# The product of the K-V sums and Wo in three f16 passes, in a one-core graph transformer layer

## What is computed

```python
xn = _layernorm(x)                                  # x: (1250, 1024)
q = relu(xn @ Wq + bq); k = relu(xn @ Wk + bk); v = xn @ Wv + bv      # 16 heads of 64
context = einsum('bhlk', q, k) / (l * 64)           # no softmax
attn = einsum('bhlk,bhkd->bhld', context, v)
mix = attn @ Wo + bo
x = x + gnn(xn) + mix                               # gnn: two graph layers over 20000 edges
x = x + ffn(_layernorm(x))                          # two quantized linear layers, gelu between
```

## Time and profile before

| | us |
|---|---|
| median of 3 runs | 1299.38 (1298.27 to 1300.58) |
| the profiled execution, whole | 1298.98 |
| its span from first to last instruction | 1297.2 |
| PE busy | 1289.7 (99%) |
| DVE busy | 848.6 (65%) |
| ACT busy | 652.1 (50%) |

### The profile page before, as it was taken

How to read it: one execution, slowest core, us unless ns; L and a number is a source line. 1 busy time by engine, 2 the same in 40 slices (tenths; PEclk the granted TensorE clock), 3 DMA queues, 4 the chain that set the end, 5 groups by cost and what they waited for, 6 DMA issues and landing times.

```text
span 1297.2 us, 18782 instructions
## 1 busy us (share of the span) xinstructions
PE 1289.7 (99%) x6370; PEld 615.0 (47%) x6370; DVE 848.6 (65%) x1472; ACT 652.1 (50%) x895; POOL 98.4 (8%) x91
## 2 busy tenths in 40 slices
PE   9999999999999999999999999999999999999999
PEld 5454445555545444444444444444444444444444
DVE  6854552362567778975992664246987978786774
ACT  7766565354312336632441763446863277465460
POOL 0000000000000001100000010133550100000000
PEclk9999999999999999999999999999999999999999
DMA  9487987864235366724877899999949829732523
GB/s 357 146 274 264 290 271 206 296 226 155 89 114 195 142 212 224 215 86 156 279 255 251 178 254 221 259 293 320 306 148 377 262 64 291 181 69 81 130 60 103
DMA packets 203094, 269.10 MB, mean 207 GB/s; under 512 B 110465, under 2 KB 144001, under 8 KB 199425
## 3 DMA queue, kind: packets, MB, share of 16 engines
q1 hardware_dynamic: 191008, 260.12, 63.5%
q0 software_dynamic: 1440, 5.24, 2.2%
q10 hardware_dynamic: 10560, 2.62, 1.3%
HBM read 184.33 MB, written 57.67 MB: 187 GB/s over the span
## 4 chain that ended last, share of the span: by engine, by line
PE 86%; DVE 6%; DMA 5%; ACT 2%; issue 1%; SPq 0%; DVEq 0%; ACTq 0%
PE ps L2366 32%; PE ps L2688 13%; PE ps L2647 12%; PE ps L2497 8%; PE ps L2768 7%; PE ps L2805 7%; PE ps L2566 3%; DMA SPLIT<-in_Wself 1%; DMA Zb<-blocks_scratch 1%; PE ps L2505 1%; PE ps L2418 1%; DVE AM L2179 1%; DMA S<-HL 1%; PE ps L2400 1%; DVE S L1859 1%
## 5 line engine op out<-in xcount | busy, mean ns | idle before, releaser
L2366 PE MATMUL ps<-S,XH 128*128 128x512 f16 x1440 | 316.7, 379 | 0.5 <-DVE Zb L1766 0.5
L2366 PEld LDWEIGHTS ps<-S,XH 128*128 128x128 f16 x1440 | 140.5, 98 | 164.4 <-DVE Zb L1766 0.6
L2366 PE MATMUL ps<-S,Zb 128*128 128x512 f16 x480 | 106.4, 379 | 0.0
L2497 PE MATMUL ps<-XH,S 128*128 128x512 f16 (+1 forms) x576 | 102.6, 339 | 0.0
L2366 PE MATMUL ps<-Zb,XH 128*128 128x512 f16 x432 | 94.8, 379 | 0.0
L1059 ACT ACTIVATE AT<-ps 128x320 f16<-128x320 f32 x40 | 17.4, 435 | 142.2 <-PE ps L2366 142.1
L1719 DVE TENSOR_SCALAR STREAM<-tables,keys 128x320 f16 x240 | 71.5, 298 | 23.5 <-PE ps L2566 13.3
L2647 PE MATMUL ps<-XH,AT 128*128 128x512 f16 x400 | 86.7, 379 | 0.0
L2647 PE MATMUL ps<-Zb,AT 128*128 128x512 f16 x400 | 86.5, 379 | 0.0
L2497 PEld LDWEIGHTS ps<-XH,S 128*128 128x128 f16 x576 | 56.1, 98 | 47.0 <-issue 2.3
L2366 PEld LDWEIGHTS ps<-S,Zb 128*128 128x128 f16 x480 | 46.9, 98 | 54.4 <-issue 0.6
(11 more groups left out here) (330 smaller groups left out, 1998.4 us busy)
## 6 DMA issues: line engine op xcount, KB each, us to landing
STREAM<-in_w_all SPq DMA_DIRECT2D x48, 512.0 KB, 5.5
STREAM<-in_w1t SPq DMA_DIRECT2D x42, 512.0 KB, 5.4
STREAM<-in_w2t SPq DMA_DIRECT2D x28, 512.0 KB, 5.1
XIN<-in_x SPq DMA_DIRECT2D x20, 512.0 KB, 5.1
Zb<-in_w1t SPq DMA_DIRECT2D x14, 512.0 KB, 7.3
blocks_scratch<-S SPq DMA_DIRECT2D x4, 1792.0 KB, 8.5
blocks_scratch<-STREAM SPq DMA_DIRECT2D x4, 1792.0 KB, 8.8
S<-blocks_scratch SPq DMA_DIRECT2D x7, 1024.0 KB, 11.4
```

The costliest lines, as they stand in the source:

```text
L2366: last = mm(acc[:, n * BANK:(n + 1) * BANK], left(l, kc), right(kc, r)[:, n * BANK:(n + 1) * BANK], start=(kc == 0 and i == 0), stop=(kc = ...
L2497: last = mm(ps[:, 3 * j * BANK + a:3 * j * BANK + b], Wq_s[:, kc, l, mc], XH[:, r, kc, a:b], start=(kc == 0 and l == 0 and r == 0), stop=( ...
```

## The change

- Wo is brought chunk by chunk through the two slots of `SPLIT` (`wo_loads`) in place of one 4 MB transfer, and split to f16 halves in `S1` by ACT (`wo_hi`) and DVE (`wo_lo`): chunks 0 and 1 ahead of Q chunk 0, 2 and 3 behind the copies to `kvT`, 4 and 5 behind Q chunk 1, 6 and 7 behind `w1_sum` on DVE and behind the means of Q chunk 1 on ACT.
- `kvT` is split too, in one piece, into `kv_parts` in `HL`, by a scale `kv_s` from its norm. ACT does its half behind the four means of Q chunk 2, DVE its half ahead of Q chunk 3.
- `m_pe` runs three f16 passes, six matmuls in place of two f32 ones. It waits for all of Wo's halves (`split_lo` 32) and both halves of `kvT` (`kvT` 17). M's own split uses the constant 2^-15.
- M(5), M(6) and M(7) move into the first U tile, ahead of its chunks 1, 2 and 4; banks and waits follow. The counts of `split_lo` that later loads wait for rise by eight.

The core of the diff:

```diff
-            sp.wait_ge(S("v_ps"), NT)
-            sp.dma_start(Wo_raw, Wo.rearrange("(k p) n -> p k n", p=P)).then_inc(S("wo_in"), 16)
+            def wo_loads(first):
+                for kc in range(first, first + 2):
+                    load_split(Wo, kc, kc % 2, 24 + kc)
+            wo_loads(0)
+            wo_loads(2)
...
-            mean_loads(0, Q_FIRST, HC)
+            for n in range(2):
+                for j in range(4):
+                    mean_load(0, Q_FIRST + 4 * n + j, j)
+                wo_loads(4 + 2 * n)
...
+            act.wait_ge(S("scales"), 4)
+            act.wait_ge(S("v_ps"), NT)
+            wo_hi(0)
             for m in range(3):
                 q_hi(m, m % 2)
...
-                if m == 2:
+                if m < 2:
+                    wo_hi(2 + 2 * m)
+                else:
                     norm("norm_m", 1, 5)
                 q_means(m)
-            act.wait_ge(S("a_m"), 1)
+                if m == 1:
+                    wo_hi(6)
+            act.wait_ge(S("kv_s"), 1)
+            A(kv_parts[:, 0, :], kvT, ACT.Copy, scale=col("kv_s")).then_inc(S("kv_hi"), 1)
...
+            wo_lo(2)
             q_dve(1, 1)
+            wo_lo(4)
...
             V.tensor_reduce(col("w1_sum"), MW[:, 0, :], AXX, ALU.add).then_inc(S("w_sum"), 1)
+            wo_lo(6)
...
+            dve.wait_ge(S("kv_hi"), 1)
+            V.scalar_tensor_tensor(kv_parts[:, 1, :], kvT, col("kv_s"), kv_parts[:, 0, :],
+                                   ALU.mult, ALU.subtract).then_inc(S("kvT"), 1)
             q_dve(3, 1)
...
-                for n in range(2):
-                    last = mm(ps[:, (bank + n) * BANK:(bank + n + 1) * BANK], kvT[:, p * P:(p + 1) * P],
-                              Wo_raw[:, p, n * BANK:(n + 1) * BANK], start=True, stop=True)
+                for i, (l, r) in enumerate(((0, 0), (0, 1), (1, 0))):
+                    for n in range(2):
+                        last = mm(ps[:, (bank + n) * BANK:(bank + n + 1) * BANK], kv_parts[:, l, p * P:(p + 1) * P],
+                                  Wo_s[:, p, r, n * BANK:(n + 1) * BANK], start=(i == 0), stop=(i == 2))
...
-            pe.wait_ge(S("wo_in"), 16)
+            pe.wait_ge(S("split_lo"), 32)
+            pe.wait_ge(S("kvT"), 17)
...
+            u_first = {1: lambda: m_late(5), 2: lambda: m_late(6), 4: lambda: m_late(7), 7: q_and_m_done}
```

More of the change, by code:

```diff
@@ L42 @@
 W_SCALE = 2.0 ** 14
+M_DOWN = 2.0 ** -15
 XW = X_SCALE * W_SCALE
@@ L117, in gps_kernel @@
             ln_std=1, ln_rstd=1, p=8, s=8, sq0=1, sq1=1, norm_kv0=1, norm_kv1=1, a_kv0=1, a_kv1=1, c_kv0=1, c_kv1=1,
-            sq_q=2, norm_q=2, sq5=5, norm5=5, bq=KC, bq2=KC, bqs=KC, a_q=1, c_q=1, kv_sq=1, w1_sum=1, norm_m=1, a_m=1,
+            sq_q=2, norm_q=2, sq5=5, norm5=5, bq=KC, bq2=KC, bqs=KC, a_q=1, c_q=1, kv_sq=1, w1_sum=1, norm_m=1, kv_s=1, a_m=1,
             c_u=1, inv=1, tmp=1, to_pos=1,
@@ L151, in gps_kernel @@
         Wv_tail = Zb[:, 2 * KC * D:2 * KC * D + 4 * D].bitcast(F32).rearrange("p (k n) -> p k n", k=2)
-        Wo_raw = S1[:, :].bitcast(F32).rearrange("p (k n) -> p k n", k=KC)
+        Wo_s = weight(S1)
+        kv_parts = HL[:, 0, :, :]
         qT = Zb[:, :].rearrange("p (h k n) -> p h k n", h=2, k=KC)
@@ L505, in u_moves @@
                 if split:
-                    load_split(Wself0, t, j, 24 + t)
+                    load_split(Wself0, t, j, 32 + t)
                 sp.wait_ge(S("u"), t + 1)
@@ L562, in _ @@
                 if t + 2 < KC:
-                    load_split(Wneigh0, t + 2, t % 2, 34 + t)
+                    load_split(Wneigh0, t + 2, t % 2, 42 + t)
                 sp.wait_ge(S("s0"), t + 1)
@@ L577, in prep_load @@
                 if n == 0:
-                    sp.wait_ge(S("split_lo"), 40)
+                    sp.wait_ge(S("split_lo"), 48)
                 elif n == 1:
@@ L1021, in m_hi @@
                 alone(act)
-                A(M_s[:, p, 0, :], banks(bank), ACT.Copy, scale=col("a_m")).then_inc(S("m_hi"), 1)
+                A(M_s[:, p, 0, :], banks(bank), ACT.Copy, scale=M_DOWN).then_inc(S("m_hi"), 1)
             def q_act(m, j):
@@ L1027, in q_act, with wo_hi @@
                 q_means(m)
+            def wo_hi(first):
+                for kc in range(first, first + 2):
+                    split_chunk(Wo_s, kc, kc % 2, 24 + kc, at("s", WO))
+            act.wait_ge(S("scales"), 4)
+            act.wait_ge(S("v_ps"), NT)
+            wo_hi(0)
             for m in range(3):
@@ L1602, in q_dve, with wo_lo @@
                                        ALU.max, ALU.subtract).then_inc(S("q_lo"), 1)
+            def wo_lo(first):
+                for kc in range(first, first + 2):
+                    split_chunk(Wo_s, kc, kc % 2, 24 + kc, at("s", WO))
+            wo_lo(0)
             q_dve(0, 0)
@@ L1674, in _ @@
             w_mean(0, ps[:, MEAN_AT + 1:MEAN_AT + 2])
[L1675 to L1679, removed]
+            pow2(col("kv_s"), col("norm_m"))
+            link(V.reciprocal(col("kv_s"), col("kv_s")))
+            V.tensor_scalar(col("kv_s"), col("kv_s"), W_SCALE, None, ALU.mult).then_inc(S("kv_s"), 1)
+            dve.wait_ge(S("kv_s"), 1)
+            times(col("a_m"), col("kv_s"), at("s", WO), M_DOWN)
             c = col("c_u")
@@ L1696, in qm_dve @@
                 q_dve(m, j)
-                m_dve(m - 3, 0 if isinstance(m, int) and m == 7 else 6)
+                m_dve(m - 3, 6)
             made = dve.alloc_register("made")
@@ L2533, in _ @@
                 qm_pe(m, m % 2)
[L2534 to L2540, removed]
+            pe.wait_ge(S("q_t"), 7)
+            pe.wait_ge(S("q_lo"), 7)
             pe.wait_ge(S("pad0"), 1)
@@ L2586, in counts_between, with m_late, q_and_m_done @@
                 return {kc: at_place(kc) for kc in {*places, *more}}
+            def m_late(p):
+                if p == 5:
+                    pe.wait_ge(S("q_t"), 8)
+                elif p == 7:
+                    pe.wait_ge(S("m_lo"), 5)
+                m_pe(p, M_BANK[p])
+            def q_and_m_done():
+                pe.wait_ge(S("q_lo"), 8)
+                pe.wait_ge(S("m_lo"), 8)
+            u_first = {1: lambda: m_late(5), 2: lambda: m_late(6), 4: lambda: m_late(7), 7: q_and_m_done}
             def u_pe(t):
                 wait(pe, "u", t - 1)
-                if t == 0:
-                    pe.wait_ge(S("m_lo"), 5)
                 product(banks(4 * (t % 2)), lambda l, p: qT[:, l, p, tile_of(t)], of(M_s), 0 if t == 0 else None, "m",
-                        counts_between(t, {7: lambda: pe.wait_ge(S("m_lo"), 8)} if t == 0 else {}))\
+                        counts_between(t, u_first if t == 0 else {}))\
                     .then_inc(S("u_ps"), 1)
@@ L2605, in s0_pe @@
                         between=counts_between(NT + t)).then_inc(S("s0_ps"), 1)
[L2607 removed]
+            pe.wait_ge(S("split_lo"), 40)
             pe.wait_ge(S("u"), 9)
@@ L2628, in deg_pe @@
                 last.then_inc(S("deg_ps"), 1)
-            pe.wait_ge(S("split_lo"), 40)
+            pe.wait_ge(S("split_lo"), 48)
             for t in range(8):
```

19 lines of the change are left out of this document (8 added, 11 removed).

## The result

The changed kernel took 1301.38 us (median of 12 runs, 1300.90 to 1304.60), the kernel before in the same sessions 1299.07 (12 runs, 1297.29 to 1300.58). The ratio is 1.0020 with a 95% interval of 1.0012 to 1.0027: **slower by 2.3 us**, 1.6 to 3.5, inside the forecast range of 1298.2 to 1303.6 and 0.4 over the forecast time. The profiled execution took 1302.64, 1.3 over the median, with a span of 1300.5, 3.3 over that of the kernel before.

What follows compares the result with a forecast made beforehand. PE, busy 99% of the span, was taken as the bound. M's gain of 3.5 us, stalls of 5.0 and a late landing of 0.1 summed to +1.6: 1301.0 us against the median, range 1298.2 to 1303.6.

Steps and rivals of the forecast that it cites:

- M's cost: M blocks on PE: 1.29 us each in place of 1.73, a gain of 3.5 us over all eight.
- The first stall: PE at total(5) in Q: waits 2.5 us for w1_sum, behind two low halves of Wo on DVE.
- The second stall: PE ahead of M(0): waits 2.5 us for kvT's halves; M(0) starts at 291.2, 5.0 later with both stalls.
- Landing of Wo chunks 6 and 7: Wo loads in Q: they land about when DVE wants their high halves; 0.1 us taken as cost.
- The rival of a late landing, (c): Wo chunk 7 in Q lands late, up to 3.8 us, giving 1304.7; chance 15%.
- The clock: PE's granted clock behind the stalls: no fall, cost taken as 0 between 0 and 14 us; a fall had 6%.
- The start of U: U's first tile: M(7) done at T (Q chunk 7's end) + 13.0, asked at T + 14.2; cost 0.
- The sum: Whole kernel: -3.5 + 5.0 + 0.1 = +1.6 us, 1301.0 against the median.
- behind U everything hangs on PE, so the shift stays as it is: Kernel behind U: PE's delay of +1.6 us is carried unchanged to the end.
- same: Whole kernel: measured within 2.6 us of no change, 1296.8 to 1302.0; chance 71%.
- (d): PE's clock falls behind one or both stalls in Q: 1.3 to 14 us more, most likely 2 to 4; chance 6%.

Runs made afterwards that it cites:

- the last pair: p_before_total against a repeat of p_after with total(5) and M(0) moved later and the count waiting for M's sixth low half: 1296.76 and 1293.32 us.
- p_total_late: p_after with total(5) and its wait for w1_sum moved 3.2 us later, into Q chunk 3: 1302.85 us.
- p_u_undone: p_after with M(5) to M(7) ahead of U again, in the banks of the kernel before: 1301.33 us.
- p_after: The changed kernel with its 74 transposing transfers replaced by plain ones of the same rows: 1301.08 us.
- p_count_6: p_after with the wait ahead of U's first count for M's sixth low half in place of its eighth: 1299.52 us.
- p_before: The kernel before the change with its 74 transposing transfers replaced by plain ones of the same rows: 1297.57 us.
- p_before_total: p_before with total(5) and its wait moved 3.2 us later, into Q chunk 3: 1296.76 us.
- the third change: On p_after with total(5) and M(0) moved later, the wait ahead of U's count is for M's sixth low half: 1293.50 us with all three.
- p_m0_late: p_after with M(0) and its waits moved 6.3 us later, into Q chunk 4: 1299.82 us.

## Why the prediction held, and where it didn't

**M's cost** was right: 1.29 per block in the profile, 3.44 in all by the last pair.

**The first stall** was right in place, releaser and size: 2.5 expected, 2.58 measured, total(5) at 275.8 expected and 275.82 measured. The step that found it was the comparison of two rows of different engines, 273.13 and 273.28, where neither showed a wait. The agreement to 0.02 us is partly luck: the chain begins one step ahead of where the prediction took it up, at ACT's first mean, which started at 259.83 here and at 259.86 in the kernel before, but up to 1.6 later in other profiles.

**The second stall** was right in what counts, 291.2 expected for M(0) and 291.26 measured, and p_total_late shows that the chain is the one that was added up. Its own size was wrong, 0.79 and not 2.5, because of the clock: 1.4 of the difference is Q chunk 3, 0.2 total(5) itself.

**Landing of Wo chunks 6 and 7** was right: ACT had made the last high half by 276.33, half a us before DVE came to it. The two low halves took 2.73 in place of 2.48, but no wait is in it: one of the two operations itself lasted 1.54 us, the other 1.27, and why stays open. The rival of a late landing didn't come about for these two; but the w1 means of p_u_undone show that a late transfer at the head of the chain delays PE directly.

**The clock** was wrong. It was a rival at 6%, with "I take 0, since the only row with idle PE time shows none". All six profiles with a stall of over 2 us in Q show the low level behind it, those without one don't. The row with 1.13 us of idle time in the earlier trace rows was too far from 2.5 to say anything. The Trainium skill, "TensorE: Matmul & The Clock Gate", section "HAM oscillation — how this bites in real kernels", warns of gaps in the matmul stream behind which the clock is granted at half. The traces agree that it happens (0.50 behind each of the six stalls), but four of these stalls, 2.25 to 2.74 us, are shorter than the gaps that its rule names; here the measurement decides. In the profile of the changed kernel the low clock did no harm to M(0), as the slow matmuls were hidden in the wait for kvT; in p_after's profile 0.7 came out.

**The start of U** is the step that failed in the sum. It said: M(7) done at T + 13.0, asked at T + 14.2, "slack 1.2", "cost 0". M(7) was done at 360.09, T + 12.9, as said, and no matmul waited for it. The cost was 3.57 - 1.66 = 1.9 us, in the count behind the wait. The working treated the wait as one of the matmuls. It is one of the sequencer. In the kernel before the low half was done at 353.4, before the sequencer came there: it went on without a wait and was 3.9 us ahead of PE at the loop's load, enough to stay ahead over three turns of 1.3. In the changed kernel it was held to 360.1, and had 1.2. p_count_6 gives 1.6 us of it back with one number changed.

**The sum**: +1.6 expected. In the profile -3.45 + 5.09 + 1.9 = +3.5 up to the first count, 3.3 at the end; by the medians +2.3. So the forecast time was near for right reasons in Q and with a term of 1.6 to 1.9 missing in U, and that it was only 0.4 off is partly luck. Two things worked against the missing term. If the kernel before waits at total(5) as p_before does, for which p_before_total gives 0.8, the loss in Q against its median is nearer 4.3 than 5.1; this is an estimate from the plain base. And "behind U everything hangs on PE, so the shift stays as it is" was wrong: two waits of 0.5 and 0.7 us took up some of it, while the one for the transfer at 886 us was 1.3 longer in the profiled execution. How these add up in the median isn't shown. The median's 2.3 us is under the 2.6 that was set as the border of "same", to which 71% were given, but the ratio's interval, 1.0012 to 1.0027, reaches over it, so the result is no test of these chances. In the range the missing term was covered by what was kept for the rivals (c) and (d).

## What to carry to other kernels

- An engine that is busy 65% can still stand in the way: before work is put on it, look at what it does in the stretch between the last thing that it waits for and the next thing that the bound engine waits for. Where no wait shows, compare the end of the one with the start of the other; a semaphore's time between them means that there is no slack.
- If such a wait can't be made earlier, let the bound engine do other work first: two waits moved 3 and 6 us later turned a loss of 3.5 us into a gain of 2.4, and with the third change of 4.1. Of this 0.8 is to be had in the kernel before too.
- A wait in the program just ahead of a loop can cost time though no matmul waits for it. Look at the sequencer's records there, not only at the engine's.
- Removing one stall of a chain gains nothing if the next one has the same end. It may lose: here the matmuls slowed behind the one long stall cost 2.9 us in full, where most of the slow time behind the first of two stalls passed in the wait of the second.

## What the runs showed of the hardware

- The granted clock fell to half (1.2 GHz) in each of six profiles in which PE stood still for 2.25 to 4.86 us in Q, and read 2.4 GHz behind single idle times of 0.7 to 2.0 us. In three of ten executions of p_m0_late it didn't fall. The matmuls behind the fall took 1.4 to 2.9 us more in all; the size differs from run to run with the same stall (1.40 behind 2.58, 2.93 behind 2.64).
- A turn of the count's loop, with its register work and its wait, takes PE's sequencer 1.3 us. Its four matmuls take 0.55 of PE (12 in 1.65). While the sequencer is ahead nothing of this is seen: with the loop's load 3.7 to 3.9 us ahead of the first matmul (the kernel before, p_count_6) the three turns cost nothing, with 1.2 (the changed kernel) 1.9 us.
